# Linear attention's opening: the first unit's gate sums ahead of tiles 6 and 7, the second batch's deviations later, four weight folds behind the first gates

## The reference

```python
y = jnp.sum(yk * topk_w[..., None], axis=1)          # yk: six rows per token, gathered from the experts' output
...
q = (h @ Wq).reshape(B, T, H, DK) * scale            # h = layernorm(x); B 4, T 512, H 8, DK 128, DV 32
k = (h @ Wk).reshape(B, T, H, DK)
v = (h @ Wv).reshape(B, T, H, DV)
gk = log_sigmoid(h @ Wgk0 @ Wgk1 + bgk1) / 16        # one gate per key channel
S = S * exp(gk_t)[..., None] + k_t[..., :, None] * v_t[..., None, :]     # step over tokens
o_t = einsum('bhk,bhkv->bhv', q_t, S)
o = o * rsqrt(mean(o * o) + eps) * g_norm_w * (g * sigmoid(g))           # g = h @ Wg
x = x + o.reshape(B, T, H * DV) @ Wo
```

## Time and profile before

| | us |
|---|---|
| median of 3 runs | 1712.09 |
| lowest and highest | 1706.8, 1718.12 |
| the profiled execution | 1702.95 |
| its span, from first to last instruction | 1700.6 |
| linear attention in it, from the first instruction of its block to the last | 292 to 662 |

### The profile page before, as it was taken

The page is one execution under the profiler, slowest core; times in us unless marked ns, Lnnn a source line. Parts: engine busy times, 40 slices in busy tenths (PEclk is TensorE's granted clock), DMA queues, the critical chain, the costliest instruction groups (busy, mean ns, idle before and its releaser), DMA issues. The chain is left out here.

```text
span 1700.6 us, 39507 instructions
## 1 busy us (share of the span) xinstructions
PE 1442.6 (85%) x14334; PEld 992.6 (58%) x14334; DVE 1081.7 (64%) x2775; ACT 736.0 (43%) x1754; POOL 774.3 (46%) x741
## 2 busy tenths in 40 slices
PE   6879997548888996898999388878999999997898
PEld 3556665424455554556666266654667777776677
DVE  6852222467775654873222488857998888874888
ACT  5533333155556533643333211116766666663121
POOL 4453332754310000554333556508998888982000
PEclk9999999669899997999999688879999999999899
DMA  8309995521100002605997222200000000000000
GB/s 264 98 14 259 293 299 147 186 78 44 48 22 1 1 1 68 183 7 161 284 304 219 81 79 77 71 1 14 3 16 3 16 4 3 16 3 3 13 17 21
DMA packets 92664, 145.50 MB, mean 86 GB/s; under 512 B 25032, under 2 KB 52528, under 8 KB 92512
## 3 DMA queue, kind: packets, MB, share of 16 engines
q1 hardware_dynamic: 62816, 93.06, 18.9%
q0 software_dynamic: 15360, 37.77, 7.3%
q10 hardware_dynamic: 14336, 12.59, 2.6%
HBM read 122.39 MB, written 18.87 MB: 83 GB/s over the span
## 5 line engine op out<-in xcount | busy, mean ns | idle before, releaser
L2290 POOL TENSOR_TENSOR sb_m_prob<-sb_m_prob,sb_m_rinv 128x512 f32<-128x512 f32 x256 | 260.4, 1043 | 44.6 <-DVE sb_m_rinv L2340 40.8
L1264 POOL DMA_INDIRECT sb_c_rows<-slot_rows,sb_slot x192 | 191.6, 998 | 107.9 <-issue 51.5
L2220 ACT ACTIVATE sb_m_prob<-m_ps_s,sb_m_nmax 128x512 f32<-128x512 f32 x256 | 173.8, 683 | 126.8 <-DVE sb_m_nmax L2346 126.2
L1098 POOL DMA_INDIRECT e_xn<-xn_rows,sb_table x128 | 118.3, 924 | 199.4 <-PE e_ps_x L1176 187.0
L1247 DVE TENSOR_TENSOR sb_e_h<-sb_e_sg,e_ps_gu 96x176 f32<-96x176 f32 x128 | 42.6, 333 | 246.7 <-ACT sb_e_sg L1223 246.7
L1185 PE MATMUL e_ps_gu<-e_wgu,sb_e_xT 128*96 128x352 f32 x512 | 176.3, 467 | 10.7 <-ACT sb_e_xT L1217 10.4
L2346 DVE TENSOR_REDUCE sb_m_nmax<-m_ps_s 128x1 f32<-128x512 f32 x256 | 163.9, 681 | 29.0 <-PE m_ps_s L2124 26.7
L2354 DVE STREAM_TRANSPOSE sb_m_pT<-sb_m_prob 128x1024 f32<-128x1024 f32 x128 | 157.6, 1232 | 0.0
L2137 PE MATMUL m_ps_v<-sb_m_pT,sb_m_lat_rows 32*64 32x128 f32 x8192 | 135.4, 274 | 5.0 <-issue 4.2
L2123 PE MATMUL m_ps_s<-sb_m_latT_high,sb_m_qa 128*128 128x512 f32 x256 | 125.5, 490 | 15.9 <-ACT sb_m_prob L2220 15.8
L2137 PEld LDWEIGHTS m_ps_v<-sb_m_pT,sb_m_lat_rows 32*64 32x64 f32 x8192 | 119.1, 130 | 28.7 <-issue 28.4
(11 more groups left out here) (281 smaller groups left out, 3083.3 us busy)
## 6 DMA issues: line engine op xcount, KB each, us to landing
e_wgu<-wgu SPq DMA_DIRECT2D x128, 352.0 KB, 4.7
e_wdn<-wdn SPq DMA_DIRECT2D x128, 192.0 KB, 4.5
slot_rows<-sb_e_y ACTq DMA_DIRECT2D x128, 96.0 KB, 4.2
xn_rows<-e_xn SPq DMA_DIRECT2D x16, 256.0 KB, 2.2
sb_c_rows<-slot_rows,sb_slot POOLq DMA_INDIRECT x192, 2.8
sb_x<-x SPq DMA_DIRECT2D x4, 512.0 KB, 5.4
e_xn<-xn_rows,sb_table POOLq DMA_INDIRECT x128, 4.9
sb_g_zm<-wqT SPq DMA_DIRECT2D x1, 2048.0 KB, 9.1
```

The costliest lines, as they stand in the source:

```text
L1098: pool.indirect_dma_start(x, None, k.xn_rows[:, :], bass.IndirectOffsetOnAxis(ap=k.table[:, e:e + 1], axis=0))\
L1264: pool.indirect_dma_start(rows[u][j][:, :], None, k.slot_rows[:, :], bass.IndirectOffsetOnAxis(ap=k.slot[:, n, j:j + 1], axis=0))\
L2220: act.activation(prob[s % 4][:, hh, :], ps_s[j % 3][:, :], ACT.Exp, bias=nmax[s % 2][:, hh:hh + 1], accum_out=rsum[s % 2][:, hh:hh + 1]).t ...
L2290: pool.tensor_tensor(part, part, rinv[s % 2][:, hh:hh + 1].to_broadcast([P, T]), ALU.mult)\
```

## The change

It moves work and changes no arithmetic:

- PE: folds 0 to 3 wait for `wqT` and `upT` alone; folds 4 to 7 come after slot -2 (after the four gates of unit 0) and wait for `wo1` there by a semaphore of its own.
- ACT: the copies of folds 4 to 7 come after `lns(0)`, ahead of `decays(0)`; in slot -1 `deviations(1)` comes after `gate_copies(0)`, just ahead of `xT_copies(1)`, instead of first.
- DVE: slot -2 becomes tiles 4 and 5, then all four gate sums and the edges of unit 0. In slot -1, tiles 6 and 7 come after the edges of unit 1, then `normalise(1)`; tiles 8 and 9 follow around the last two scales.
- POOL and SP issue what they issued, in the same order.

```diff
         def _(sp):
-            for dst, name in ((wqT, "wqT1"), (upT, "upT1"), (wo1, "wo1")):
+            for dst, name in ((wqT, "wqT1"), (upT, "upT1")):
                 sp.dma_start(dst, k.w[name].rearrange("(h p) d -> p h d", p=DH)).then_inc(raw_loaded, 16)
+            sp.dma_start(wo1, k.w["wo1"].rearrange("(h p) d -> p h d", p=DH)).then_inc(out_loaded, 16)
...
-            pe.wait_ge(raw_loaded, 48)
-            for n in range(FOLDS):
+            pe.wait_ge(raw_loaded, 32)
+            for n in range(ABSORBS):
                 fold(n)
             transposes(0)
             low_rank(0)
             pe.wait_ge(w_low, 1)
-            for u in range(-2, U):
+            slot(-2)
+            pe.wait_ge(out_loaded, 16)
+            for n in range(ABSORBS, FOLDS):
+                fold(n)
+            for u in range(-1, U):
                 slot(u)
...
             def slot(u):                                # ACT
-                if b_in is not None:
+                if b_in is not None and u >= 0:
                     deviations(b_in)
...
                     lns(u + 2)
+                if u == -2:
+                    for n in range(ABSORBS, FOLDS):
+                        fold_copy(n)
...
                 if b_in is not None:
+                    if u < 0:
+                        deviations(b_in)
                     xT_copies(b_in)
...
-            for n in range(FOLDS):
+            for n in range(ABSORBS):
                 fold_copy(n)
...
             def slot(u):                                # DVE
-                if u == -2:
-                    add_rows(4, range(TOPK))
-                    statistics(4)
-                    add_rows(5, range(TOPK))
-                    statistics(5)
...
-                if b_in is not None:
+                if b_in is not None and u >= 0:
                     normalise(b_in)
...
-                add_rows(n, range(4))
+                if u >= 0:
+                    add_rows(n, range(4))
...
-                add_rows(n, range(4, 6))
-                statistics(n)
+                if u >= 0:
+                    add_rows(n, range(4, 6))
+                    statistics(n)
...
                 gate_sums(u + 2, range(3, 4))
                 edges(u + 2)
+                if u == -1:
+                    for early in (6, 7):
+                        add_rows(early, range(TOPK))
+                        statistics(early)
+                    normalise(b_in)
                 scale(u + 1, 6)
...
-                add_rows(n + 1, range(3))
+                add_rows(n if u == -1 else n + 1, range(3))
...
                 scale(u + 1, 7)
-                add_rows(n + 1, range(3, 6))
+                if u == -1:
+                    add_rows(n, range(3, 6))
+                    statistics(n)
+                    add_rows(n + 1, range(TOPK))
+                else:
+                    add_rows(n + 1, range(3, 6))
                 statistics(n + 1)
...
             low_parts(0)
-            for u in range(-2, U):
+            for n in (4, 5):
+                add_rows(n, range(TOPK))
+                statistics(n)
+            gate_sums(0, range(HG))
+            edges(0)
+            for u in range(-1, U):
                 slot(u)
```

More of the change, by code:

```diff
@@ L1310, in linear_attention @@
                                               k.sem("g_normed_ready"))
-    raw_loaded, fold_ready, fold_free = k.sem("w_fold_loaded"), k.sem("w_fold_ready"), k.sem("w_fold_free")
+    raw_loaded, out_loaded, fold_ready, fold_free = k.sem("w_fold_loaded"), k.sem("w_out_loaded"), k.sem("w_fold_ready"), k.sem("w_fold_free")
     made = k.sem("g_constants_made")
```

## The result

| | before | after |
|---|---|---|
| median of 20 runs each, us | 1709.49 | 1718.05 |
| lowest and highest | 1701.26, 1719.09 | 1711.74, 1729.72 |
| the profiled execution, its span | 1702.95, 1700.6 | 1715.85, 1714.1 |

The ratio is 1.005, with a 95% interval of 1.0032 to 1.0068: the changed kernel is slower by 8.6 us (5.5 to 11.6 by the interval), where +8.3 was forecast.

What follows compares the result with a forecast made beforehand. The opening up to slot 0's first gate was taken as the bound: 7.3 us won at unit 1's gates, but late tiles 8 and 9 move its end from 395.42 to 403.7, +8.3; from 1712.09 this gives 1720.4, range 1708 to 1730.

Steps and rivals of the forecast that it cites:

- Clock at the head: PE idles after folds 0 to 3, then does batch 0's transposes and low-rank product at low clock: net +1.1 us.
- Folds behind the gates hidden: Folds 4 to 7 run in PE's idle stretch behind unit 0's gates: no cost, at worst 0.5 us.
- Unit 1's gates earlier by 7.3: Unit 0's sums ahead of tile 6 let unit 1's gate parts on ACT start at 360.1, 7.3 us earlier.
- Tile 6 behind unit 1's edges at 378.6: DVE reaches tile 6 at 378.6 instead of 351.69, after unit 1's edges; its rows end at 381.7.
- Gathers: POOL fetches tile 8 from 382.6; twelve issues, last landing 399.2; DVE waits, low part ends 403.7 against 395.42: +8.3 us.
- The second chain: Tile 7's statistics through batch 1's transposes and two key projections, then tiles 8 and 9: low part at 402.2.
- Even prompt gathers would leave +6.8: Without any wait for tiles 8 and 9's gathers, the second chain alone would still delay the opening's end by 6.8 us.
- Size: The whole kernel shifts with slot 0's first gate, by +8.3 us: 1720.4 from the median 1712.09.
- faster: Rival: the 7.3 us won at unit 1's gates reach the end, 1704.8, needing tile 9 by 385; chance 0.07.
- Slower by 1%: Rival: PE idles before slot 0's first gate and stays at 1.2 GHz through the slot, +16.6 us, 1728.7; chance 0.10.
- No shift: Rival: a wait in slot 0 independent of its first gate takes up part, +0 to +4 us; chance 0.10.

Runs made afterwards that it cites:

- e5: The changed kernel with tiles 8 and 9 gathered into spare buffers, so POOL needn't wait for tiles 6 and 7; 1711.33 us, ratio to before 1.001.
- e4: The changed kernel with tiles 6 and 7 early, batch 1 prepared before unit 1's last sums, tile 9 in slot 0; 1700.15 us, ratio to before 0.9959.
- e1: The changed kernel with tile 6 directly behind unit 0's edges and tile 7 behind unit 0's second query scale; 1704.42 us, ratio to before 1.0001.
- e2: The kernel before with only the move of folds 4 to 7 behind slot -2; 1708.87 us, ratio to before 1.0019.
- e6: The changed kernel with batch 1's low part directly behind tile 8 and tile 9's rows between slot 0's first scales; 1707.12 us, ratio to before 1.0001.
- e7: e4 with all eight folds back at the head of PE's and ACT's queues; 1699.09 us, ratio to before 0.9939.
- e3: The changed kernel with all eight folds back at the head of PE's and ACT's queues; 1715.64 us, ratio to before 1.006.

## Why the prediction was right, and where its terms were off

The forecast came out in its size and by its mechanism; that the medians agree with it to 0.3 us is in part luck, as the point on size says. Point by point, with distances from tile 3 so that the two executions compare:

- **Clock at the head.** As said: in the changed kernel PE idles ahead of the first transposes (14.13 us) and does batch 0's low-rank product in 3.75 us, against 1.96; I had taken 3.5. Two windows of the changed kernel (columns as in rows 1, with DMA share and GB/s last):

```profile
328.00:332.00 4.00, 0.00 (x0) 0.00 (x0) 3.29 (x8) 0.30 (x1) 3.08 (x4) 0.50 0.35 100
332.00:340.00 8.00, 5.72 (x12) 2.70 (x12) 1.60 (x5) 2.34 (x6) 6.17 (x7) 0.50 0.39 109
```

  The granted clock is 0.50 throughout, the lower of the two levels. Unit 0's logarithms end 22.08 us after tile 3 starts (349.85 - 327.77) against 20.54 (347.33 - 326.79): +1.5 where I said +1.1 with a bound of 1.6.
- **Folds behind the gates hidden.** Right; the cover was 0.47 us thin.
- **Unit 1's gates earlier by 7.3.** 361.38 is 33.61 after tile 3, before it was 40.64: -7.0.
- **Tile 6 behind unit 1's edges at 378.6.** Too early by 1.8 us: 53.63 after tile 3, where my time stands for 51.81. I had set DVE's sums and scales of slot -1 at their pitch of one pair; two key scales waited for PE besides, one of them the 1.61 at 376.58, the other 0.33.
- **Gathers.** The wait on the buffer (0.86 for 0.87) and the landing (2.77 for 2.8) held; the twelve issues took 14.43 us (399.77 - 385.34) instead of 13.8, because four of them took 1.06 to 1.21 rather than 0.95. DVE waited for tile 9's, as said.
- **The second chain.** "Even prompt gathers would leave +6.8": e5 is that case, and left +8.92 in the trace, 1.8 below the changed kernel where the two ends of my sum lay 1.5 apart. Its extra 2.1 is mostly the 1.8 of tile 6. In e5 the issues are what takes POOL's time: (376.64 - 362.14) / 11 = 1.32 us from one to the next. The Trainium skill, "DMA: Bandwidth & Descriptors", section "Anatomy of one DMA — SWDGE (gpsimd) path", calls descriptor generation small. The measured pitch stands against that; what I had drawn from the page, that the second chain alone would leave most of the loss, is what e5's trace shows.
- **Size.** The two traces show +10.7 at slot 0's first gate against my +8.3; 1.8 is the late tile 6 and 0.6 the longer issues. The medians show +8.6, so part of the traced pair's excess belongs to those two executions: they differ by 12.9 us in all. Nor did the rest of the layer keep its old length in them: it took 2.6 us more. A sum that was 2.4 short at the gate in the trace and 0.3 off in the medians was lucky in the second.

Of the rivals, "faster" failed because its condition did: tile 9 is not in place by 385, it lands at 402.5. e4 gives tile 9 another place and normalises earlier, and there 7.74 us are won at the gate, with tile 9's 3.8 among the reasons. So what stood behind the gap decided. "Slower by 1%", PE staying at the low level through slot 0, failed: four passes of the first projection took 3.62 us, the next four 2.20, against 1.96 at the high level. The granted clock was 0.50 up to 412 and 0.93 from there to 414. "No shift" failed by the +13.3 at the last `sb_g_on`.

That no other part of the changed order costs anything rests on the sum of e1 and e2. For ACT's late deviations the trace settles it, though they were not moved alone. ACT's timeline of the changed kernel, the first of the two activations:

```profile
389.08 0.30 ACT L1631 ACTIVATE sb_g_ln_var<-sb_g_mv,sb_eps 128x4 f32<-128x4 f32 x1 [13.20 <-DVE sb_g_mv L1820]
```

ACT stood idle for 13.20 us ahead of it, until DVE had tile 7's statistics, so here their later place in ACT's queue held nothing up.

Between the first gate and the last `sb_g_on` every kernel loses something more against the kernel before, from 0.4 us (e6) and 0.9 (e5) to 2.6 (changed) and 3.4 (e7), in a single execution each. Part of it is slot 0's restart at a lower clock (last section): to the first output product the changed kernel takes 1.05 us more than the kernel before, e7 1.61 more, e6 1.43 less. For what is left, 0.4 us in e5 and 1.4 to 1.9 in the others, I have no cause.

## What to carry to other kernels

When work is moved behind a wait to shorten it, follow what the moved work itself releases: here a buffer whose release starts fifteen microseconds of gather issues, and a batch whose normalised tokens PE needs. A gap's length tells what can be won there, but the win arrives at the end only if every other chain to the same point is shortened too; price them all, since the second was within two microseconds of the first. The cheap repair is to find which part of the late work nobody at that point needs (tile 9) and let the awaited instruction pass it.

## What the runs showed of the hardware that was not expected

- The price of a restart of PE isn't told by the idle time in front of it alone. From slot 0's first gate to the first output product (`g_ps_o<-sb_g_atm`) it took 9.08 us before, after 1.72 of idleness; 10.11 in e2 after 1.79; 7.65 in e6 after 1.52, where the first gate ran in 0.50 us, at the high level, instead of 0.80; 10.13 in the changed kernel after 7.45; 9.59 in e5 after 5.29. The granted clock over the 8 us from that gate does tell it: the nine traces come in the same order by clock and by distance, from 1.00 (e6) over 0.82 (before), 0.79 (e4, 9.36), 0.75 (e5) and 0.68 (changed) to 0.61 (e7, 10.69). Windows of the kernel before, of the changed one and of e6 (columns as above):

```profile
395.47:403.47 8.00, 8.00 (x20) 4.01 (x20) 2.08 (x3) 4.68 (x8) 5.87 (x7) 0.82 0.35 99
407.19:415.19 8.00, 8.00 (x17) 4.07 (x18) 2.07 (x3) 3.62 (x6) 5.88 (x7) 0.68 0.34 99
403.24:411.24 8.00, 7.57 (x36) 3.78 (x36) 4.72 (x9) 5.52 (x10) 6.33 (x7) 1.00 0.32 91
```

- Folds at the head don't ensure the high clock for batch 0's low-rank product. In e3 and e7 PE had worked on all eight folds until some 4 us before, and the product took 3.23 and 3.65 us against 1.96 in the kernel before. The granted clock of e3, in windows with the columns as above, goes from the high level to the low one within it:

```profile
336.00:338.00 2.00, 1.21 (x8) 0.80 (x8) 1.38 (x4) 0.99 (x5) 1.58 (x2) 1.00 0.41 121
338.00:340.00 2.00, 1.32 (x4) 0.59 (x3) 0.00 (x0) 0.62 (x2) 1.51 (x2) 0.85 0.32 88
340.00:342.00 2.00, 2.00 (x3) 0.34 (x1) 0.00 (x0) 0.00 (x0) 1.39 (x3) 0.50 0.34 109
```

  In the kernel before it stayed at 1.00 through the same product, after the same folds; I have no cause for the difference:

```profile
334.93:336.89 1.96, 1.96 (x4) 0.65 (x4) 0.00 (x0) 0.00 (x0) 1.35 (x3) 1.00 0.29 96
```
